# Turned keys for odd score steps, and an accumulating DMA for the bias, in a windowed-attention layer on eight cores

## What is computed

```
q = x @ Wq + bq ; k = x @ Wk + bk ; v = x @ Wv + bv
out = softmax(q . k over 256 keys) @ v
x = layernorm(x + out @ Wo + bo)
xr, xk = mixes of x with the row before it
x = layernorm(x + sigmoid(xr @ Wr) * (relu(xk @ Wk)^2 @ Wv))
```

## Time and profile before

| | |
|---|---|
| Time, median of 3 runs (range) | 510.87 us (510.54 to 511.59) |
| Profiled execution, device time | 509.77 us |
| Its slowest core and span | core 5, 508.2 us |
| Spans of all cores | 504.9 to 508.2 us |
| PE, ACT, DVE, POOL busy (share of span) | 87%, 66%, 62%, 21% |
| Mean granted clock of the TensorE, core 5 | 0.960 |
| Products issued | 3,052 |

### The profile page before, as it was taken

How to read it: one execution, slowest core, us unless ns; L and a number is a source line. 1 busy time by engine, 2 the same in 40 slices (tenths; PEclk the granted TensorE clock), 3 DMA queues, 4 the chain that set the end, 5 groups by cost and what they waited for, 6 DMA issues and landing times.

```text
span 508.2 us, 10503 instructions; the slowest of 8 cores (504.9 to 508.2 us)
## 1 busy us (share of the span) xinstructions
PE 440.9 (87%) x3052; PEld 220.6 (43%) x3052; DVE 316.5 (62%) x793; ACT 333.3 (66%) x847; POOL 109.0 (21%) x298
## 2 busy tenths in 40 slices
PE   0779999999899869798898988998979988999990
PEld 0344444444444345444363353353435345464640
DVE  0056765654655587576967877877776896545421
ACT  1267868686768575776679496669658769446542
POOL 4330124130403030101122230121123032130303
PEclk9996999999999878899999999999989999999996
DMA  8999429939263646100265286567254548303112
GB/s 108 164 164 195 62 44 115 161 64 140 28 110 54 113 73 117 40 5 1 66 139 135 52 100 156 110 84 187 53 115 115 135 53 177 90 1 103 43 42 83
DMA packets 71448, 48.25 MB, mean 95 GB/s; under 512 B 59104, under 2 KB 60256, under 8 KB 71392
## 3 DMA queue, kind: packets, MB, share of 16 engines
q0 software_dynamic: 11632, 24.88, 28.1%
q1 hardware_dynamic: 59760, 22.70, 22.7%
HBM read 40.85 MB, written 8.39 MB: 97 GB/s over the span
## 4 chain that ended last, share of the span: by engine, by line
PE 59%; ACT 15%; DVE 9%; issue 8%; DMA 5%; POOL 1%; ACTq 0%; SPq 0%; DVEq 0%; POOLq 0%
PE pm L289 11%; PE pm L276 8%; PE pm L319 8%; PE pm L309 6%; PE pm L301 6%; PE po L344 6%; ACT p L383 5%; PE psc L231 4%; DVE nmax L529 4%; PE pm L255 3%; DMA bufq<-wq 2%; PE pm L291 2%; ACT junk L464 2%; DMA yT<-qy 2%; PE pm L270 1%
## 5 line engine op out<-in xcount | busy, mean ns | idle before, releaser
L383 ACT ACTIVATE p<-psc,nmax 128x320 bf16<-128x320 f32 x264 | 138.8, 540 | 96.1 <-DVE nmax L529 95.9
L529 DVE TENSOR_REDUCE nmax<-psc 128x2 f32<-128x640 f32 x132 | 108.1, 821 | 88.8 <-PE psc L237 88.2
L289 PE MATMUL pm<-w16o,ao 128*128 128x512 bf16 x272 | 66.3, 388 | 2.5 <-ACT ao L441 1.2
L541 DVE TENSOR_SCALAR p<-p,rall 128x320 bf16<-128x320 bf16 x264 | 62.4, 299 | 7.6 <-DVE rall L534 0.7
L276 PE MATMUL pm<-bufx,bufq 128*128 128x512 bf16 (+2 forms) x320 | 65.1, 350 | 1.7 <-DMA bufq<-wq 1.7
L301 PE MATMUL pm<-bufx,w16kf 128*128 128x256 bf16 x512 | 62.4, 278 | 2.1 <-ACT pt L397 1.5
L309 PE MATMUL pm<-w16r,bufx 128*128 128x512 bf16 x256 | 59.6, 379 | 5.0 <-DVE zx L565 2.2
L319 PE MATMUL pm<-w16vf,bufq 128*128 128x512 bf16 x256 | 59.5, 380 | 1.8 <-ACT pt L397 1.8
L383 ACT ACTIVATION_READ_ACCUMULATOR p<-psc,nmax 128x1 f32 x264 | 57.1, 216 | 0.0
L301 PEld LDWEIGHTS pm<-bufx,w16kf 128*128 128x128 bf16 x512 | 48.7, 99 | 14.1 <-issue 8.0
L231 PE MATMUL psc<-k,qy 64*128 64x320 bf16 x264 | 41.7, 313 | 13.5 <-ACT p L383 13.1
(11 more groups left out here) (80 smaller groups left out, 572.4 us busy)
## 6 DMA issues: line engine op xcount, KB each, us to landing
zx<-xres POOLq DMA_DIRECT2D x17, 512.0 KB, 6.3
out<-zb SPq DMA_DIRECT2D x16, 512.0 KB, 3.2
bufx<-xt POOLq DMA_DIRECT2D x16, 256.0 KB, 8.9
bufq<-wq POOLq DMA_DIRECT2D x4, 512.0 KB, 10.0
w16o<-wo POOLq DMA_DIRECT2D x8, 256.0 KB, 11.8
w16kf<-wkf POOLq DMA_DIRECT2D x8, 256.0 KB, 5.8
w16r<-wr POOLq DMA_DIRECT2D x8, 256.0 KB, 6.1
w16vf<-wvf POOLq DMA_DIRECT2D x8, 256.0 KB, 6.5
```

Of the source, the lines that this page charges most:

```text
L289: e.matmul(pm[:, bank, :], ao[:, a % 2, kc, :], w16o[:, kc, 512 * b:512 * b + 512], start=(kc == 0), stop=False)
L383: a = e.activation(p16[:, b % 2, j // 2, g, j % 2, :], psc[:, 2 * (n % 2) + g, 0:320], AF.Exp, bias=nmax[:, n % 4, g:g + 1], accum_out=sal ...
L529: e.tensor_reduce(nmax[:, n % 4, :], psc[:, 2 * (n % 2):2 * (n % 2) + 2, 0:320], mybir.AxisListType.X, ALU.max, negate=True).then_inc(s_mx, 1)
L541: t = e.tensor_scalar(part, part, rall[:, b % 2, r:r + 1], None, ALU.mult)
```

## The change

Three parts.

1. **Keys.** For the odd steps (j odd) the 320 keys are not read from `k16` but from a copy `kr`, turned by 64: keys 256 to 319 first, then 0 to 255. DVE makes the copy of blocks 0 to 4, POOL that of blocks 5 to 32 (`turn_keys`, two copies for a block, of 256 and 64 columns, in slot 4b - 4), two buffers; `qk` waits for it in step j = 1. The mask of an odd step goes to the first and second 64 columns.
2. **Value product.** Chunk c + 3 now holds the odd step's keys that chunk c holds of the even step, and both halves of chunk 2 hold keys 256 to 319. So `av` issues eight products in place of twelve: a pair of 512 columns, a pair of 256 with rows 0 to 63, a pair of 512, and a pair of 256 with rows 64 to 127.
3. **Bias.** The 34 products with `ones` go. The bias comes as a 128-row f32 array. SP loads it into `zx` (0.5 MB each time): for tiles 0 and 1 right at the start, for tile tau + 2 in slot `YOUT` + 1 after a wait for `s_y`. POOL then waits for that load (`d_bo`) and adds the residual rows by an accumulating DMA, one slot later than it loaded them before.

```
+            if j == 1 and b < KD:
+                e.wait_ge(s_kd, b + 1)
+            if j == 1 and b >= KD:
+                e.wait_ge(s_kp, b - KD + 1)
...
+                keys = kr[64 * g:64 * g + 64, b % 2, :] if j % 2 else k16[64 * g:64 * g + 64, 64 * b:64 * b + 320]
...
-                mm = e.matmul(pm[:, bank, :], ones[:, :], bo16[:, 512 * b:512 * b + 512],
-                              start=False, stop=True)
...
+            for g in range(2):
+                both(g, 0)
+            for g in range(2):
+                mm = last_keys(g, 0)
+            mm.then_inc(s_lo, 1)
+            for g in range(2):
+                both(g, 1)
+            e.wait_ge(s_lo, b + 1)
+            for g in range(2):
+                mm = last_keys(g, 1)
             mm.then_inc(s_av, 1)
...
+        def add_xres(tau):
+            e.wait_ge(d_bo[tau % 2], 16 * (tau // 2 + 1))
+            e.dma_start(zx[:, tau % 2, :], xres.ap()[128 * tau:128 * tau + 128, :],
+                        accum_op=ALU.add).then_inc(d_xres[tau % 2], 16)
...
+        def turn_keys(b):
+            e.wait_ge(s_ea, ACT_COUNT[INDEX[("K", key_group(b), 0)]])
+            e.wait_ge(s_qk, 4 * b - 4)
+            if b == KD:
+                e.wait_ge(s_kd, KD)
+            e.tensor_copy(kr[:, b % 2, 64:320], k16[:, 64 * b:64 * b + 256])
+            e.tensor_copy(kr[:, b % 2, 0:64], k16[:, 64 * b + 256:64 * b + 320]).then_inc(s_kp, 1)
...
-            if n - 1 in YOUT[:NT - 2]:
-                tau = YOUT.index(n - 1)
-                e.wait_ge(s_y, tau + 1)
-                e.dma_start(zx[:, tau % 2, :], xres.ap()[128 * (tau + 2):128 * (tau + 3), :]) \
-                    .then_inc(d_xres[tau % 2], 16)
+            if n - 2 in YOUT[:NT - 2]:
+                add_xres(YOUT.index(n - 2) + 2)
...
     def sync(e):
         e.dma_start(cols[:, :], cols_in.ap()).then_inc(d_cols, 16)
+        for j in range(2):
+            e.dma_start(zx[:, j, :], bo_in.ap()).then_inc(d_bo[j], 16)
...
+            if n - 1 in YOUT[:NT - 2]:
+                tau = YOUT.index(n - 1)
+                e.wait_ge(s_y, tau + 1)
+                e.dma_start(zx[:, tau % 2, :], bo_in.ap()).then_inc(d_bo[tau % 2], 16)
```

More of the change, by code:

```diff
@@ L30 @@
 GSLOT = (None, 8, 24, 36, 48)
+KD = 5
 BT = 18
@@ L191, in build_nc @@
     mur_s, muk_s = cols[:, 12:20], cols[:, 20:28]
-    d_cols, d_mask, d_ident, d_bo = sem("d_cols"), sem("d_mask"), sem("d_ident"), sem("d_bo")
+    d_cols, d_mask, d_ident = sem("d_cols"), sem("d_mask"), sem("d_ident")
+    d_bo = [sem("d_bo%d" % j) for j in range(2)]
     d_wk, d_wv, d_wo = sem("d_wk"), sem("d_wv"), sem("d_wo")
@@ L336, in av, with last_keys, both @@
                 e.wait_ge(s_ao, b)
[L337 to L350, removed]
+            def last_keys(g, half):
+                lo, hi = 64 * half, 64 * half + 64
+                vc = k + r + 2 if half == 0 else k + 2
+                return e.matmul(po[64 * g:64 * g + 64, :].rearrange("p (s k q) -> p k s q", k=2, q=128)[:, half, :, :],
+                                v16[lo:hi, (b + half) % 2, vc, 64 * g:64 * g + 64],
+                                pt[lo:hi, r, :, g, 2, :],
+                                start=False, stop=(half == 1), tile_position=(lo, 64 * g), skip_group_check=True)
+            def both(g, c):
+                return e.matmul(po[64 * g:64 * g + 64, :].rearrange("p (s k q) -> p s k q", k=2, q=128),
+                                v16[:, r, k + r + c, 64 * g:64 * g + 64],
+                                pt[:, r, :, g, c:c + 4:3, :],
+                                start=(c == 0), stop=(c == 1), tile_position=(0, 64 * g), skip_group_check=True)
+            for g in range(2):
[8 more added lines that the diff above has]
+                mm = last_keys(g, 1)
             mm.then_inc(s_av, 1)
@@ L610, in vector @@
                 max_step(n + 1)
+            b, i = divmod(n + 4, 4)
+            if 2 <= b < KD and i == 0:
+                turn_keys(b)
             b, i = divmod(n - 1, 4)
@@ L828, in _host_inputs @@
     w = np.arange(64)[None, :]
-    mask = np.stack([np.where(w >= r, 0.0, -BIG), np.where(w < r, 0.0, -BIG)], 1).astype(np.float32)
+    first, last = np.where(w >= r, 0.0, -BIG), np.where(w < r, 0.0, -BIG)
+    mask = np.stack([first, last, first], 1).astype(np.float32)
     shared = dict(
@@ L838, in _host_inputs @@
         wvf=_by_chunks(np.asarray(L0_ffn_W_v, np.float32).T),
-        bo=np.ascontiguousarray(np.asarray(L0_attn_bo, np.float32).reshape(1, D)),
+        bo=np.ascontiguousarray(np.tile(np.asarray(L0_attn_bo, np.float32).reshape(1, D), (128, 1))),
         mask=mask,
```

42 lines of the change are left out of this document (25 added, 17 removed).

## The result

The changed kernel takes 520.89 us (median of 4 runs, 517.77 to 521.30) against 510.71 us of the kernel before, run beside it: a ratio of 1.0187, interval 1.0143 to 1.0231. It is slower by about 10 us, outside the predicted range. The profiled execution took 521.3 us with a span of 519.6 us. In some executions of any of these kernels a die runs at a lower clock and the time is longer; the ratios leave such runs out and the medians of all runs take them in, so where the two differ the ratio counts.

What follows compares the result with a forecast made beforehand. PE was taken as the engine with least room, 59% of the chain of waits. -11.3 + 2.2 + 0 + 1.5 + 2 = -5.6 us from 509.77 gives 504.2, median 505.3 us; range 498.5 to 512.5 us, about 0.8.

Steps and rivals of the forecast that it cites:

- Bias products removed: PE, 34 bias products at 0.41 us each, about 32 on the chain: 11.3 us less, bounds 7 and 13.9.
- Value product: PE, 33 blocks: merged product takes 1.08 us against 1.01, one more row change; +2.2 us, bounds -8 and +5.5.
- The rival in which the product gains: PE's value product: cheaper row changes or per-product overhead give -4 us there, 497.4 us in all; chance 0.12.
- Keys, 0: Turned key copies on DVE and POOL, made four slots ahead, are covered: 0 us, bounds 0 and +2.
- Start, +1.5: Two first bias loads (1 MB) push back inputs of PE's first product: 1.5 us later, bounds 0 and 3.2.
- Bias loads and POOL's wait, +2 net: Tiles 2 to 16: POOL's wait delays layer norms, less a transpose wait that goes; +2 us, bounds -3 and +10.
- The expected compensation: Near tile 9 the residual load no longer runs beside the transposes, so DVE's 3.43 us wait for `yT` goes.
- slower: POOL's queue: Rival: POOL's bias wait holds layer norm scales that ACT needs; 13 us there, 516.3 us in all; chance 0.17.
- point of decision (7.6 us): Size of the cost of POOL's bias wait from which the slower rival decides the outcome.
- Gain absorbed: Rival: PE's saved time becomes waits for ACT and DVE; bias worth only 7 us, 509.6 us; chance 0.18.
- clock: Rival: another stretch of lowered PE clock after waits, some 2 us each, inside the range; no chance given.
- the signs that it named against itself: Value product under 0.95 us; PE waits for `kr`; first product at 14 or beyond 17; POOL waits above 8; PE idle +5.

Runs made afterwards that it cites:

- e3: Kernel before with its 34 bias products left out and nothing in their place (output lacks the bias): 500.97 us.
- e5: Kernel before with its bias products kept but given 128 contraction rows in place of one: 507.79 us.
- e2: Changed kernel with the bias left out altogether and the residual loaded plainly, so only turned keys and shared value product remain changed: 503.17 us.
- e9: Changed kernel with SP's two first bias loads issued only when the x of the second group has landed: 515.16 us.
- e15: Changed kernel with the two first bias loads late and the three early y transposes together behind tile 4's bias load: 510.85 us.
- e13: e15 with POOL's bias wait and accumulating load, from tile 6 on, three slots later and behind that slot's layer norm: 501.50 us.
- e10: Changed kernel with the y transposes of tiles 0 to 2 right behind the bias loads of tiles 2 to 4: 516.26 us.
- e11: Changed kernel with POOL's bias wait and accumulating load three slots later, behind that slot's layer norm, for all tiles loaded in slots: 520.38 us.
- e1: Kernel before with the bias part of the change alone, keys and value product as before: 520.07 us.
- e4: Kernel before without bias products; POOL loads the residual plainly and adds the bias by an accumulating DMA four slots later: 519.72 us.
- e8: Changed kernel without bias loads or the wait for them, the residual still loaded by accumulating DMA (output lacks the bias): 502.44 us.
- e6: Kernel before without bias products; POOL adds the bias to the landed residual by one tensor_tensor per tile: 508.24 us.

## Why the prediction was wrong

The forecast was 505.3 us; 520.9 came. By its own steps:

- **Bias products removed, -11.3.** Measured -9.4 (e3), inside the bounds of 7 and 13.9 and on the side where part of it is absorbed. The two gaps, 0.2 us together, are confirmed by e5. L291 is gone, as foreseen.
- **Value product, +2.2.** 1.13 us and not 1.08: the step from a 512-column pair to the 64-row pair is 0.34 us, where I took 0.213 + 0.10; the way back, 0.22 to 0.23, is as I had it. 33 x 0.12 = 4.0 us on PE, of which about 2.3 reach the end (e2 less e3). The rival in which the product gains had no part.
- **Keys, 0.** Right: nobody waits for `kr`, and POOL's copies (515 and 330 ns on the mean) lie in idle time.
- **Start, +1.5.** Mis-sized: 3.4 us on the slowest cores of the two traces, past the upper bound of 3.2 (2.9 on the median of their cores), and 4.9 to 5.7 in the run without it. I took two loads to cost 3.2 us of the engines and let half of it fall into idle time. It did not: the key weights landed 8.9 us after their issue in this trace, and after 4.8 us with the bias loads away (e9), so they were held back by 4.1 us, and the x pieces behind them.
- **Bias loads and POOL's wait, +2 net.** This step failed. It was put at "bounds -3 and +10" and was 12 to 14 us, SP's order included: 17.4 us for the whole bias part, less the start. It had the right mechanism at the right tile, and priced it as ACT's wait of 3.5 us, with a transpose's wait to set against it. Two sizes were wrong. POOL's waits for the bias loads are 6.9 us each (97.1 over 14), not 3: at tile 9 SP issues the load behind two transposes, and it lands 5.0 us later and not 3.7. And a wait of ACT was taken as its price: ACT's was 5.3 us, PE's behind it 6.1, and PE then worked at half its clock. e15 less e13 puts the mechanism at 9.4 us. The expected compensation came at its place only: DVE has no wait for `yT` near 310 us in the changed kernel (3.43 us before), but its waits for `yT` in all rose from 17.4 to 19.1 us.
- **What the prediction left out: SP's order.** It asked what is behind POOL's new wait and did not ask the same of SP: `wait_ge(s_y, tau + 1)` in front of each bias load stands in front of the y transposes of tiles 0 to 2. In the kernel before SP had nothing to wait for in between and issued them as soon as their tiles were ready, at 77.28, 86.74 and 110.96 us and not from 165.89 on (timeline of SP in the kernel before, which merges them with the next two):

```profile
77.28 107.02 SPq L747 DMA_TRANSPOSE yT<-qy  x5
```

e10 gives 4.6 us back by moving them; e15 less e9, which differ in their place alone, says 4.3 by the medians, 4.1 by the ratios. In e11 these transposes cost 14.1 us, so that the late accumulate's gain behind them does not show.

So the rival "slower: POOL's queue" (516.3 us, chance 0.17) was the mechanism, with a point of decision (7.6 us) that was passed. That even its sum comes within 4.6 us is in part luck: it put 13 us on POOL's wait, which measured 9.4, and nothing on SP's order, which measured 4 to 5, and too little on the start. Its argument against itself, that POOL is needed early only where a second layer norm is due, was true and no comfort: ACT waited at three of the five places that it named (tiles 9, 11 and 14: 5.3, 2.8 and 3.5 us). At tile 9 PE's wait behind it was longer than ACT's (6.1 us); at tile 11 it was not (2.65 us). Gain absorbed and clock were no cases of their own; the clock is part of the price of each stall.

Of what was to show it: copies nobody waits for, L291 gone, the wait for `yT` gone and ACT waiting for POOL near 300 us all came. Of the signs for it, the value product (1.13 us for 1.08), the first product (17.47 us for 15.5) and POOL's waits (6.9 us each for 3) missed. Of the signs that it named against itself three came: the first product beyond 17 us, waits for POOL above 8 us in all (13.5), and PE's idle time from 50 to 457 us grown by 407.0 - 363.0 - 33.2 = 10.8 us.

What stays open: why e1 and the changed kernel are level though their keys differ by 2 us in every other pair, why e11's transposes take so much longer, and what in e4 beyond the two places named makes up its 19 us.

## What to carry to other kernels

A wait that is added to a queue costs what stands behind it in the written order, on every queue that gets one: list, for the issuing engine as much as for the waiting one, which later instruction used to run ahead, and move the wait behind it. Here the same loads, bytes and waits cost 18 to 19 us in one order (the changed kernel less e13, by ratio and medians) and nothing that can be measured in another. Take edits back together as well as singly, and read where each gains and loses: the late accumulate alone won some 9 us from tile 9 on and lost 10 at the transposes before them (the table above, e11 against the changed kernel), and its time showed nothing.

## What the runs showed of the hardware that I had not expected

- An accumulating DMA of 512 KB lands 1.3 us later than a plain one and takes 0.28 us more to issue (medians; a 4 KB packet 328 ns for 159), and the kernel takes no longer for 15 of them (e8 against e2).
- 8.9 MB of additional DMA traffic, placed behind what is urgent, cost nothing that can be measured (e13 against e8), while 1 MB of it at the start cost 3.4 us to the first product of the slowest core.
- A product with one contraction row costs 0.2 us more than the same with 128 rows between neighbours of 128 rows (e5).
- A stall of 6 us on PE costs more than itself: eight products behind it took 3.57 us in place of 1.73, at a granted clock of 0.50.
- DVE's bf16 normalisation of 128x320 takes 0.299 us alone and 1.03 us on the mean while POOL adds two f32 tiles of 128x1024; a maximum out of PSUM is not touched (e6).
